# Four fused cross-attention layers on one core: order of the first transfers, and E copies shared by two engines

## The reference, cut to what matters

```
x = L0(ctx, x)   # 16 heads of 16: keys and values from ctx and x (256 tokens), masked; out + residual, rmsnorm, MLP 256-1024-256 with gelu
x = L1(x, ctx)   # 32 query heads, 8 key heads of 8; additive mask; out + residual, layer norm
x = L2(x, ctx)   # RWKV block: token shift, five low-rank mixes, a recurrence over tokens with 8x8 states, group norm, gate, channel mix
x = L3(x, ctx)   # 16 heads of 16 over the normed ctx, boolean mask; x + tanh(gate) * out
```

```
scores = einsum('bhtd,bhsd->bhts', q, k) * scale      # masked
attn = softmax(scores, axis=-1)
out = einsum('bhts,bhsd->bhtd', attn, v)
```

## Time and profile before

| | us |
|---|---|
| median of three runs | 1126.52 |
| lowest and highest | 1123.29, 1128.92 |
| the profiled execution, whole | 1128.1 |
| its span, first to last instruction | 1126.1 |
| TensorE busy (matmuls) | 980.3, 87% |
| VectorE busy | 806.4, 72% |
| ScalarE busy | 739.1, 66% |
| GpSimd busy | 256.7, 23% |

### The profile page before, as it was taken

One profiled execution on the slowest core, in us unless ns is written; L12 is line 12 of the kernel. 1 busy time (PEld: TensorE's weight loads), 2 busy tenths in 40 slices (PEclk: granted clock), 3 DMA queues, 4 the chain that ended last, 5 costly groups with the idle time before them and its releaser, 6 DMA issues.

```text
span 1126.1 us, 23973 instructions
## 1 busy us (share of the span) xinstructions
PE 980.3 (87%) x7776; PEld 699.8 (62%) x7776; DVE 806.4 (72%) x3113; ACT 739.1 (66%) x2675; POOL 256.7 (23%) x349
## 2 busy tenths in 40 slices
PE   5779898998999899998999899998999899888356
PEld 4456566765766577665767577665766577556144
DVE  3408758886878776977878777987878776966623
ACT  1828853887658973788658983887658973881116
POOL 3102304031320413032321413031311413120300
PEclk9889999999999999999999999999999999989576
DMA  9100000000010000000010001000010000000000
GB/s 303 41 1 17 6 1 24 2 8 2 2 33 8 2 2 20 16 8 1 2 33 8 2 2 28 7 8 2 1 33 8 2 2 10 2 3 10 0 1 10
DMA packets 18091, 18.90 MB, mean 17 GB/s; under 512 B 7216, under 2 KB 16432, under 8 KB 17712
## 3 DMA queue, kind: packets, MB, share of 16 engines
q1 hardware_dynamic: 17968, 17.37, 5.1%
HBM read 15.27 MB, written 2.10 MB: 15 GB/s over the span
## 4 chain that ended last, share of the span: by engine, by line
PE 60%; DVE 14%; ACT 10%; issue 6%; POOL 2%; POOLq 0%; DVEq 0%; ACTq 0%
PE ring L678 16%; PE ring L688 15%; PE ring L730 9%; PE psS L719 5%; ACT E L1029 5%; DVE S L1213 3%; PE psO L764 2%; PE psO L772 2%; PE ring L897 2%; PE ring L669 2%; PE psO L805 2%; PE ring L887 1%; DVE slot L1389 1%; PE psS L788 1%; DVE SS L1432 1%
## 5 line engine op out<-in xcount | busy, mean ns | idle before, releaser
L1029 ACT ACTIVATE E<-S,nmax 128x128 f32<-128x128 f32 (+1 forms) x1024 | 423.7, 419 | 32.4 <-PE ring L730 21.3
L1213 DVE CUSTOM_DVE_ANT_0 S<-psS,mb 128x128 f32<-128x128 f32 (+1 forms) x1024 | 263.0, 319 | 39.8 <-ACT E L1029 17.2
L678 PE MATMUL ring<-slot,w_l 128*128 128x256 f32 x992 | 243.9, 393 | 16.5 <-ACT slot L990 12.3
L730 PE MATMUL ring<-ident,E 128*128 128x128 f32 x1280 | 202.3, 289 | 29.5 <-ACT E L1029 25.3
L678 PEld LDWEIGHTS ring<-slot,w_l 128*128 128x128 f32 x992 | 185.5, 195 | 54.8 <-ACT slot L990 14.6
L730 PEld LDWEIGHTS ring<-ident,E 128*128 128x128 f32 x1280 | 144.9, 145 | 101.8 <-ACT E L1029 63.0
L1029 ACT ACTIVATION_READ_ACCUMULATOR E<-S,nmax 128x1 f32 x1024 | 195.6, 191 | 0.0
L688 PE MATMUL ring<-w_l,slot 128*128 128x256 f32 (+1 forms) x640 | 155.1, 387 | 12.1 <-DVE slot L1453 4.7
L688 PEld LDWEIGHTS ring<-w_l,slot 128*128 128x128 f32 x640 | 116.3, 196 | 42.5 <-issue 8.8
L1016 ACT ACTIVATE ET<-ring 128x512 f32<-128x512 f32 x192 | 106.9, 587 | 17.2 <-PE ring L730 17.1
L719 PE MATMUL psS<-keys,slot 32*128 32x512 f32 (+1 forms) x768 | 97.3, 580 | 21.4 <-ACT ET L1016 12.8
(11 more groups left out here) (120 smaller groups left out, 1131.7 us busy)
## 6 DMA issues: line engine op xcount, KB each, us to landing
slot<-in_ctx SPq DMA_DIRECT2D x8, 256.0 KB, 2.8
slot<-in_x SPq DMA_DIRECT2D x8, 256.0 KB, 2.8
w_l<-in_wl SPq DMA_DIRECT2D x1, 2048.0 KB, 10.7
out<-slot SPq DMA_DIRECT2D x8, 256.0 KB, 2.1
w_l<-in_wl SPq DMA_DIRECT2D x2, 768.0 KB, 6.6
w_l<-in_wl SPq DMA_DIRECT2D x1, 1152.0 KB, 8.5
m0i<-in_m SPq DMA_DIRECT2D x8, 128.0 KB, 3.1
mb<-in_m SPq DMA_DIRECT2D x8, 128.0 KB, 2.5
```

The costliest lines, as they stand in the source:

```text
L678: m = pe.matmul(b[:, a, :], w[:, k, m0 + a * P:m0 + (a + 1) * P], src[:, k, :], start=(k == 0), stop=(k == kt - 1))
L730: m = pe.transpose(b[:, k, :], E[:, g % RING_E, k * P:(k + 1) * P], ident[:, :])
L1029: ins = act.activation(E[:, g % RING_E, h * w:(h + 1) * w], S[:, g % RING_S, h * w:(h + 1) * w], ACT.Exp, bias=nmax[:, g % 4, h:h + 1], sc ...
L1213: ins = dve.tensor_tensor_reduce(S[:, g % RING_S, h * w:(h + 1) * w], psS[g % QUAD][:, h * w:(h + 1) * w], bias[:, bb, :], -1.0, HUGE, ALU ...
```

## The change

**Transfers.** Context, tokens and mask of the first pair are issued first. The weights q, k and v of layer 0 come apart, each with a semaphore of its own, with the table of columns between k and v; then the two rows of biases that the values need, the weights of layer 1, the gate, and the other rows once v is in. Each engine waits only where it uses them: TensorE in `q0`, `k0l`, `k0c`, `v0c`, `v0l` of the phase `start`, ScalarE and VectorE for the columns, VectorE in its value copies for rows and cleared buffers.

**E copies.** Of attentions 0 and 3 the copies of odd jobs go to VectorE, in every turn: 8 of 16 and 4 of 8. `weigh` of a pair of jobs waits for both engines.

**Constants and waits.** `spread_j` shrinks from eight matrices to two, made by one copy; the constants of layer 2 are made in the step `cols` of the phase `first`; tanh of the gate moves behind `aT` of that phase. The waits for score banks and for `psO` are now taken from a list `STAGES`, by the stage that used them before.

**Order.** All four tables are written anew, with the same steps.

```diff
-EMPTIES.update({("turn", layer, n): {0: "A", 1: "D", 3: "A"}[layer] for layer in NJ for n in range(NJ[layer])})
+EMPTIES.update({("turn", layer, n): "D" if layer == 1 or n % 2 else "A" for layer in NJ for n in range(NJ[layer])})
...
-@start xT cT q0 k0l k0c v0c v0l k1 v1 @first scores0.0 aT turn0.0 scores0.4 turn0.1 turn0.2 turn0.3 weigh0.1 scores0.8
+@start cT xT q0 k0l k0c v1 v0c v0l k1 @first scores0.0 aT turn0.0 scores0.4 turn0.1 turn0.2 turn0.3 weigh0.1 turn0.4
...
+STAGES = {"start": [], "first": [0, 1], "second": [0, "r", 1], "steady": [0, 3, "r", 1],
+          "closing": [0, 3, "r", 1], "last": [3, "r"], "end": [3]}
...
         def _(sp):
-            sp.dma_start(W0t[:, 0:qkv], wl0[:, 0:qkv]).then_inc(s_w, 16)
-            sp.dma_start(colt[:, :, :], cols).then_inc(s_w, 16)
-            sp.dma_start(rowt[:, :, :], rows.partition_broadcast(P)).then_inc(s_w, 16)
-            sp.dma_start(gate_t[:, 0:1], gate.partition_broadcast(P)).then_inc(s_w, 16)
...
             program("start", None)
+            sp.dma_start(W0t[:, 0:CT * C], wl0[:, 0:CT * C]).then_inc(s_wq, 16)
+            sp.dma_start(W0t[:, CT * C:2 * CT * C], wl0[:, CT * C:2 * CT * C]).then_inc(s_wk, 16)
+            sp.dma_start(colt[:, :, :], cols).then_inc(s_w, 16)
+            sp.dma_start(W0t[:, 2 * CT * C:qkv], wl0[:, 2 * CT * C:qkv]).then_inc(s_wv, 16)
+            for n in (ROWS.index("v0_b"), ROWS.index("v1_b")):
+                sp.dma_start(rowt[:, n:n + 1, :], rows[:, n:n + 1, :].partition_broadcast(P)).then_inc(s_row, 16)
             sp.dma_start(W1t[:, :], wl1).then_inc(s_w1, 16)
+            sp.dma_start(gate_t[:, 0:1], gate.partition_broadcast(P)).then_inc(s_gate, 16)
+            sp.wait_ge(s_wv, 16)
+            sp.dma_start(rowt[:, 1:len(ROWS) - 1, :], rows[:, 1:len(ROWS) - 1, :].partition_broadcast(P)).then_inc(s_rows, 16)
...
         def _(pe):
-            pe.wait_ge(s_setup_d, 4)
-            pe.wait_ge(s_w, WEIGHTS_IN)
+            pe.wait_ge(s_const, 2)
...
-                    turned = ("turn", layer, n)
-                    pe.wait_ge(leaves(turned), left(turned))
+                    for m in (n,) if layer == 1 else (n - 1, n):
+                        pe.wait_ge(leaves(("turn", layer, m)), left(("turn", layer, m)))
...
         def _(act):
-            act.wait_ge(s_w, WEIGHTS_IN)
             act.wait_ge(s_const, 3)
-            act.activation(gate_t[:, 1:2], gate_t[:, 0:1], ACT.Tanh).then_inc(s_setup, 1)
+            act.wait_ge(s_w, 16)
...
-            for j in range(8):
-                at = lane_at(j)
-                dve.tensor_copy(spread_j[:, j, :].rearrange("p (a b) -> p a b", b=8),
-                                ident[:, at:at + 16].unsqueeze(2).to_broadcast([P, 16, 8]))
...
+                    dve.tensor_copy(spread_j[:, :, :].rearrange("p a (h d) -> p (a h) d", d=8),
+                                    mod32[:, :].unsqueeze(2).to_broadcast([P, 32, 8]))
```

More of the change, by code:

```diff
@@ L384, in phase_before, with stage_before @@
     return earlier, TIMES["steady"] - 1 if earlier == "steady" else None
+def stage_before(phase, i, stage):
+    k = STAGES[phase].index(stage)
+    while k == 0:
+        if phase == "first":
+            return None
+        phase, i = phase_before(phase, i)
+        k = len(STAGES[phase])
+    return phase, i, STAGES[phase][k - 1]
 def job_before(phase, i, g, back):
@@ L783, in spread_v @@
                     else:
[L784 removed]
+                        score_banks_free("r")
                     for a in range(2):
```

500 lines of the change are left out of this document (263 added, 237 removed).

## The result

The changed kernel takes **1174.89 us** (median of 4 runs, 1173.62 to 1179.35) against 1127.72 us of the kernel before on the same chip: a ratio of **1.0419, 95% interval 1.0356 to 1.0481**. It is 47 us slower. The forecast was 1107.0 us, its range ended at 1127, and slower had a chance of 0.12.

A forecast was written before the change was run, and what follows sets the result against it. TensorE was taken as busiest, its winnable idle time being waits for ScalarE in attentions 0 and 3 and at both ends. Terms -5.0, -3.5, -13, +4, -2 sum to -19.5: 1108.6 us, 1107.0 against the median; range 1085 to 1127.

The forecast's parts named there:

- the +4 for VectorE's load: Steady turns: TensorE's waits for VectorE, 14.5 us in the four largest, grow by a quarter, +4 us.
- the -13: Steady turns: half of TensorE's 25.9 us of waits for ScalarE go, -13 us, bounds 0 and -25.9.
- 85% of 128.4: Steady turn: VectorE rises by 7.9 to 108.7 of 128.4 us, staying below TensorE's 119.8.
- The argument against the slower rival: Attention 1: TensorE waits only 1.8 us for 124 ET copies already on VectorE between masks, 0.015 us each.
- the slower rival: VectorE's in-order queue becomes the bound: 96 copies each hold TensorE back 0.4 us, +38.4, giving 1141.4 us; chance 0.15.
- It decides from 0.25 us a copy: Moved copies: the delay of TensorE per copy at which 96 copies cancel 23.5 us of gains.
- The last turns (-2): Two attentions 3 nearly alone: 8 copies go to VectorE, 4 leave ScalarE's final chain; -2 us, bounds 0 and -4.
- The second step that failed: All four programs: the new order holds the same steps, so it got no term, only making -13 and +4 possible.
- The start: Before the first scores: reordered transfers let q0 start near 7.7 instead of 12.78 us; -5.0, bounds -1 and -6.9.
- The first attention: First turn's attention 0: 8 of 16 copies leave ScalarE, 4.4 us of its work; -3.5 us, bounds 0 and -4.4.
- The signs: Start, first attention, turns and waits: expected turns of 125 to 126 us; wrong if turns stay at 128 or more.
- The rule of the Trainium skill: Whole kernel: VectorE is the engine to relieve; 63 us of added copies come on top, 1190 us; chance 0.02.

The follow-up runs named there:

- the added work: Old order tables with the new start, all copies on ScalarE, VectorE making 96 additions nobody waits for where the moved copies would stand: 1159.32 us, ratio 1.0288.
- the split: Old order tables with the new start, the 96 odd copies of attentions 0 and 3 moved from ScalarE to VectorE: 1151.07 us, ratio 1.0183.
- experiment 1: The changed kernel with the four old order tables and all E copies of attentions 0 and 3 back on ScalarE: 1126.53 us, ratio 0.9991.
- the split alone: Old order tables with the new start, only the 8 odd copies of the first turn's attention 0 on VectorE: 1123.84 us, ratio 0.9962.
- the split with window A's order: Old order with 96 copies on VectorE, steps between attention 0's first and last transposes in the changed kernel's order, 8 of 9 turns: 1169.44 us.

## Why the prediction was wrong

**The step that failed first** is the +4 for VectorE's load ("grow with its load. I take a quarter"). With the -13 it made a gain of 9 for the middle turns; in the old order the copies that move there cost 14.7 us (attention 0) and 5.3 (attention 3, with the last turns). The reading under it was that idle time is room: "85% of 128.4" of a turn, and "VectorE has 320 idle us". All moved copies stand in the stretch of attentions 0 and 3, where the earlier trace rows has VectorE busy for 47.7 of 60 us; the 12 copies at 0.656 make it 55.6 of 60, 93%, and not 85. But even a share by stage would not have told it, since VectorE was busy for only 76% of attention 0 (166.8 of 219.0 us) and the 22.3 us added there made the stage 21.6 longer. The wait that the term left out is that of the masks behind the added work: ScalarE's wait for nmax grew from 7.8 to 26.6 us.

**The argument against the slower rival failed** with it. TensorE waited 0.015 us a copy in attention 1, and that did not carry over to attention 0; why attention 1 is so tolerant was not tested. The rival said "It decides from 0.25 us a copy", before gains; the runs gave 21.6 to 24.5 us over 96 copies, 0.23 to 0.26, with all gains already taken off, so more than 0.25 before them. Its mechanism was half of it: the copy behind the mask (21.6 us), and the mask behind the copy, which it did not have. Its time, 1141.4, fell short because it kept all gains of the forecast and had no price for the order.

**The -13 was probably too large.** "Half gone" of 25.9. The three waits for ScalarE fell by 7.9 us with the split, a quarter of 30.8, and the difference between the added work and the split is about 8 us as well, though not sharply. The 12.8 us of the scores' wait did not go with the split (12.9) but with the order. The last turns (-2) did not show: the split and the new order there together give nothing measurable, though an effect of 2 us would be hard to see.

**The second step that failed:** "The order of all four programs is new. Its effect is not a term of its own, since the two lists hold the same steps". It cost 24 us on top of the split, as much as the split. That is shown by the two kernels that differ only in the tables. Of the places, one is known: the transpose of the recurrence's output, which waits 7.7 us for VectorE instead of 1.2. The rest stays open.

**The start**, -5.0: 2.55 at q0 and 2.08 at the first scores in the changed kernel, 1.5 in experiment 1, and between 0 and 3 in the time. Two causes were missed. The table of columns landed 1.25 us later than summed (2.3 in experiment 1), and ScalarE's table load, 1.28 us, which the prediction put at "nothing", lost its cover: ahead of tanh it had run while the tokens were awaited.

**The first attention**, -3.5: 1.4 with the split alone, and in the changed kernel 24.9 us, 0.8 more than before; the split with window A's order, 27.8 us, says that the new order took it back. Its bounds, 0 and -4.4, held for the split.

**The signs.** Of those that the prediction named, the first transposes before 6 us, ScalarE level with TensorE in the first attention and VectorE's 108 us came. Turns of 135.3 us and TensorE's waits for VectorE's copies (9.5, 4.8 and 4.2 us) were the signs of being wrong.

**The rule of the Trainium skill** in Perfetto Trace Analysis, section Identifying the Most-Contended Engine, which puts VectorE (72%) before TensorE (weight loads 62%) here, was given 0.02 in its full form, 1190 us. The runs side with its direction: VectorE's added busy time counts nearly in full in attention 0, and about half of it over the program.

## What to carry to other kernels

Idle time of the engine that receives work is not room for it, neither over the turn nor over the stage, when the engine is a link in a loop with the others. The test is a run: add work, and take the stage's length less that engine's busy time. If it stays the same, you are adding to the loop. Before work is moved, put a dummy of its length at the same place on the receiving engine; that one run (33 us here) gives the order of the price without building the move. Choose a dummy that reads and writes the same memories as the real work, since this one slowed its neighbours too. An order written anew is a change by itself: time it with the old assignment, and the assignment with the old order. And where an order moves work between stages, compare idle time and not the stages' lengths.

## What the hardware showed

**TensorE ran part of attention 0 at 1.2 GHz instead of 2.4.** In the seven attentions 0 of the kernel before TensorE's instructions take 187.7 us, with the added work 203.0 for the same matmuls (x246 and x247 in the turn shown), at a granted clock of 0.84 instead of 1.00 in that turn. TensorE's idle time in these stages rose from 31.3 to 42.0 us, its busy time by 15.3: more than half of the 26 us by which they grew is slower matmuls. Two stretches inside the turn shown, with added work:

```profile
642.00:648.00 6.00, 3.23 (x28) 1.22 (x27) 4.84 (x22) 3.65 (x13) 3.81 (x5) 0.77 0.00 0
648.00:655.00 7.00, 6.14 (x44) 4.67 (x44) 6.17 (x30) 4.08 (x13) 2.22 (x3) 0.50 0.01 2
```

The clock fell in a stretch of which TensorE was idle for nearly half, and stayed at the lower level while it was busy again for 6.1 of 7 us. The sum of idle time alone does not decide it: the split old order has more of it in these stages (44.7 us), a clock of 0.88 to 1.00, and 8.2 us of slower matmuls.

**VectorE's addition of two buffers in SBUF slows beside GpSimd.** It takes 0.69 us alone; 16 of the 96 take from 0.97 to 1.53 us, all of them beside a GpSimd operation on 128x512 (mean of all 96: 0.752). GpSimd's 14 operations of the turn shown rise from 11.5 to 12.8 us; with the copies out of PSUM they stay at 11.4, and none of those copies takes more than 0.70. The Trainium skill (GPSIMD Engine Reference, section Specifications) names contention with VectorE's instructions that have two inputs in SBUF; the trace agrees. Timeline of VectorE and then GpSimd in the kernel with added work:

```profile
635.38 0.69 DVE L1333 TENSOR_TENSOR pad<-pad 128x512 f32<-128x512 f32 x1
...
642.80 1.07 DVE L1333 TENSOR_TENSOR pad<-pad 128x512 f32<-128x512 f32 x1
```

```profile
641.59 1.73 POOL L1669 TENSOR_TENSOR slot<-slot,rowt 128x512 f32<-128x512 f32 x1
```
